# Two-layer deformable-attention kernel: the feed-forward steps and the next segment's preparation at other steps of the hand-written order

## What is computed

```
q    = grouped 1x1 of bn1(x)
off  = tanh(1x1 of gelu(6x6 stride-4 depthwise conv of q)) * 4      # 64 sample points a group
kv   = bilinear sample of bn1(x) at grid + off;  k, v = grouped 1x1 of kv
pos  = query grid - sample points;  f = sign(pos) * log1p(|pos|)    # 1024 x 64 x 2 a group
bias = w3 . relu(w2 . relu(w1 . f + b1) + b2) + b3                  # hidden width 32
attn = softmax(q.k * scale + bias);  x = x + out_w . (attn . v) + out_b
x    = x + mlp_w2 . gelu(mlp_w1 . bn2(x) + mlp_b1) + mlp_b2         # 128 -> 512 -> 128
```

## Time and profile before

| | before |
|---|---|
| median of 3 runs (lowest to highest) | 901.86 us (900.08 to 902.5) |
| the profiled execution: its time / span of its instructions | 902.57 us / 900.7 us |
| busy in the span: PE / ACT / DVE / POOL | 812.3 / 676.0 / 714.7 / 69.1 us |
| ACT_TABLE_LOADs, in all | 28 of 1283 ns |
| DMA queue of the kernel, share of 16 engines | 10.4% |
| TensorE's granted clock, mean | 0.979 |

### The profile page before, as it was taken

How to read it: one execution, slowest core, us unless ns; L and a number is a source line. 1 busy time by engine, 2 the same in 40 slices (tenths; PEclk the granted TensorE clock), 3 DMA queues, 4 the chain that set the end, 5 groups by cost and what they waited for, 6 DMA issues and landing times.

```text
span 900.7 us, 27769 instructions
## 1 busy us (share of the span) xinstructions
PE 812.3 (90%) x12470; PEld 232.4 (26%) x12470; DVE 714.7 (79%) x498; ACT 676.0 (75%) x775; POOL 69.1 (8%) x40
## 2 busy tenths in 40 slices
PE   2299998899999999788999999988999999999997
PEld 1122222222222222222222222222222222222224
DVE  4699798898876688989885868889888668989843
ACT  1368777978786687896877777797777677888863
POOL 2120013210000004030000000302000000000000
PEclk8589999999999999999999999999999999999999
DMA  4310101020020101002020100102002010100000
GB/s 150 80 30 25 28 9 45 7 53 4 14 54 14 50 3 50 9 3 55 3 64 15 49 4 3 50 8 53 4 4 64 14 50 2 50 27 2 2 15 24
DMA packets 23510, 26.77 MB, mean 30 GB/s; under 512 B 15328, under 2 KB 17504, under 8 KB 23392
## 3 DMA queue, kind: packets, MB, share of 16 engines
q1 hardware_dynamic: 23392, 24.99, 10.4%
HBM read 22.79 MB, written 2.08 MB: 28 GB/s over the span
## 4 chain that ended last, share of the span: by engine, by line
PE 42%; issue 39%; ACT 9%; DVE 5%; POOL 5%; DMA 1%; SPq 0%; ACTq 0%; POOLq 0%
PE pair L887 14%; PE scores L905 13%; ACT h L484 5%; PE pair L861 4%; DVE h L638 3%; POOL conv_prod L356 3%; PE pair L1040 2%; POOL big L464 2%; PE scores L916 2%; PE pair L995 1%; PE pair L1013 1%; PE pair L1031 1%; PE scores L1001 1%; ACT big L586 1%; PE pair L940 1%
## 5 line engine op out<-in xcount | busy, mean ns | idle before, releaser
L638 DVE TENSOR_TENSOR h<-hx,hy 128x2048 f32<-128x2048 f32 x256 | 582.1, 2302 | 76.5 <-PE pair L887 72.4
L484 ACT ACTIVATE h<-pair 128x1024 f32<-128x1024 f32 x512 | 517.6, 1024 | 146.9 <-PE pair L861 104.7
L887 PE MATMUL pair<-h,wts 32*32 32x512 f32 x8192 | 300.6, 605 | 20.5 <-DVE h L638 6.1
L905 PE MATMUL scores<-h,wts 128*32 128x512 f32 x2048 | 275.7, 607 | 0.1
L861 PE MATMUL pair<-fy,u_rows 32*128 32x512 bf16 x1024 | 102.6, 387 | 17.1 <-DMA fy<-fy_dram 17.1
L887 PEld LDWEIGHTS pair<-h,wts 32*32 32x32 f32 x8192 | 66.0, 103 | 82.2 <-ACT h L484 34.7
L861 PEld LDWEIGHTS pair<-fy,u_rows 32*128 32x128 bf16 x1024 | 26.4, 91 | 234.4 <-issue 234.4
L905 PEld LDWEIGHTS scores<-h,wts 128*32 128x32 f32 x2048 | 42.2, 108 | 158.0 <-issue 149.2
L356 POOL TENSOR_TENSOR conv_prod<-qpad,wts 128x288 f32<-128x288 f32 x16 | 34.0, 2153 | 417.7 <-ACT qpad L511 417.7
L464 POOL TENSOR_TENSOR big<-big,hat_x 128x512 f32<-128x512 f32 x16 | 32.4, 2054 | 126.6 <-DVE big L736 126.6
L995 PE MATMUL pair<-const,probs 128*128 128x128 f32 x128 | 20.6, 284 | 21.6 <-ACT h L484 20.8
(11 more groups left out here) (101 smaller groups left out, 375.0 us busy)
## 6 DMA issues: line engine op xcount, KB each, us to landing
hx<-features_dram SPq DMA_DIRECT2D x64, 128.0 KB, 2.7
hy<-features_dram SPq DMA_DIRECT2D x64, 128.0 KB, 3.1
wts<-weights_dram SPq DMA_DIRECT2D x2, 960.0 KB, 8.4
att_den<-reciprocals_dram SPq DMA_DIRECT2D x7, 256.0 KB
x<-x_dram SPq DMA_DIRECT2D x2, 512.0 KB, 5.7
fy<-fy_dram SPq DMA_DIRECT2D x64, 6.0 KB
fy<-fy_dram SPq DMA_DIRECT2D x64, 4.0 KB
fy<-fy_dram SPq DMA_DIRECT2D x64, 2.0 KB
```

Of the source, the lines that this page charges most:

```text
L484: emptied("z", 2 * g + j, act.activation(h2[j][g % H2_BUFS][:].rearrange("p r n -> p (r n)"), pair_of("z", 2 * g + j)[:], ACT.Relu))
L638: dve.tensor_tensor(h1[g % H1_BUFS][:].rearrange("p c (y x) -> p c y x", x=W), hx[unit % 2][:, :, t].unsqueeze(2).broadcast_to([128, CT, H ...
L887: ins = pe.matmul(z_of(g, r)[32 * c:32 * (c + 1)], w(l, "w2")[key_rows(r), key_rows(r)], h1[g % H1_BUFS][key_rows(r), c], start=r >= 2, st ...
L905: ins = pe.matmul(scores[phase % 2][32 * r:32 * (r + 1)], w(l, "w3")[:, 32 * t:32 * (t + 1)], h2[rows[0] // 2][step % H2_BUFS][:, r % 2], ...
```

## The change

Two of the tables get other numbers, and the entries of the perceptron become a table of their own with three rows, so that the two query halves of a segment can have different steps. Arithmetic, tiles and instructions stay the same.

```diff
 BEFORE_SLOTS = {
-    ("dve", "norm1", 0): 28, ("pe", "q", 0): 28, ("act", "q_out", 0): 28, ("pool", "conv_products", 0): 31,
+    ("dve", "norm1", 0): 32, ("pe", "q", 0): 32, ("act", "q_out", 0): 32, ("pool", "conv_products", 0): 35,
...
 AFTER_SLOTS = {
     ("pe", "attend", 0): 5, ("act", "attend_out", 0): 5, ("dve", "reciprocal", 0): 9, ("dve", "divide", 0): 12,
-    ("pe", "project", 0): 12, ("dve", "residual1", 0): 14, ("pe", "mlp_up", 0): 14, ("act", "mlp_gelu", 0): 14,
-    ("pe", "mlp_up", 1): 15, ("act", "mlp_gelu", 1): 15, ("pe", "mlp_down", 0): 17, ("dve", "residual2", 0): 19,
+    ("pe", "project", 0): 12, ("dve", "residual1", 0): 14,
 }
+MLP_SLOTS = [{
+    ("pe", "mlp_up", 0): up, ("act", "mlp_gelu", 0): up, ("pe", "mlp_up", 1): up + 1, ("act", "mlp_gelu", 1): up + 1,
+    ("pe", "mlp_down", 0): down, ("dve", "residual2", 0): down + 2,
+} for up, down in ((21, 27), (15, 21), (14, 17))]
...
-        for (engine, stage, part), step in AFTER_SLOTS.items():
+        mlp = MLP_SLOTS[2 if half >= LAST - 1 else half % 2]
+        for (engine, stage, part), step in [*AFTER_SLOTS.items(), *mlp.items()]:
```

More of the change, by code:

```diff
@@ L76 @@
 BEFORE_SLOTS = {
-    ("dve", "norm1", 0): 28, ("pe", "q", 0): 28, ("act", "q_out", 0): 28, ("pool", "conv_products", 0): 31,
[L78 to L87, removed]
+    ("dve", "norm1", 0): 32, ("pe", "q", 0): 32, ("act", "q_out", 0): 32, ("pool", "conv_products", 0): 35,
+    ("pool", "conv_products", 1): 35, ("dve", "conv_products", 0): 35, ("dve", "conv_products", 1): 36,
+    ("pe", "image_t", 0): 35, ("act", "image_t_out", 0): 35, ("dve", "conv_sum", 0): 37,
+    ("dve", "conv_sum", 1): 38, ("act", "conv_gelu", 0): 37, ("pe", "offset", 0): 38,
+    ("act", "offset_tanh", 0): 38, ("dve", "positions", 0): 41, ("pe", "spread", 0): 40,
+    ("act", "features", 0): 40, ("act", "spread_out", 0): 40, ("dve", "features_sign", 0): 43,
+    ("act", "distances", 0): 42, ("act", "distances", 1): 43, ("act", "distances", 2): 44,
+    ("act", "distances", 3): 45, ("dve", "hats", 0): 46, ("dve", "hats", 1): 48,
+    ("pool", "hat_products", 0): 46, ("pool", "hat_products", 1): 48, ("dve", "hat_products", 0): 49,
+    ("dve", "hat_products", 1): 50, ("pe", "sample", 0): 52, ("dve", "sample_out", 0): 54,
+    ("pe", "keys_values", 0): 55, ("act", "keys_values_out", 0): 55,
 }
@@ L130, in plan @@
     parts = {}
-    for (engine, stage, part) in list(BEFORE_SLOTS) + list(AFTER_SLOTS):
+    for (engine, stage, part) in [*BEFORE_SLOTS, *AFTER_SLOTS, *MLP_SLOTS[0]]:
         parts[engine, stage] = max(parts.get((engine, stage), 0), part + 1)
```

## The result

The changed kernel takes **902.79 us** (median of 12 runs, 901.41 to 906.0) against 901.84 (12 runs, 900.08 to 903.15): a ratio of 1.0019, 95% interval 1.001 to 1.0027. That is within 0.3%, if anything slightly slower, and not the forecast 897.8. The profiled execution took 902.18 us with a span of 900.4.

A forecast was written before the change was run, and what follows sets the result against it. PE sets the pace in undisturbed phases, so an ACT load counts only where PE waits for ACT. Per segment -0.2 - 0.8 - 1.0 + 1.3 - 0.9 = -1.6, three times -4.8 from 902.57: 897.8 us; range 890.5 to 904.

The forecast's parts named there:

- The gain is eaten in steps 42 to 50: Rival: crowded steps 43 and 44 delay the last hats, POOL's products hold h tiles; +0.5 a segment, 901 to 904; chance 0.23.
- Preparation, DVE and POOL: I take 0, in between: Hats to last products: POOL's products may each hold an h tile 1.08 us; bounds -1.9 to +2.1 a segment, taken as 0.
- the sign that the prediction had named for this: Phase 6 or 7: PE waiting over 2 us a segment for DVE's h tiles would show the DVE term wrong.
- Perceptron, -0.2: Phases 1 to 3: one Gelu wait gone, -0.4; less cover at steps 14 and 16, +0.2; together -0.2 us a segment.
- one wait of PE for Gelus: Sign: PE's waits at L892 for Gelus would be one of about 0.4 us a segment, at step 14.
- step 12's load: Step 12's Exp loses its table load, taken as hidden behind a `project` on PE: 0, up to -0.8 us.
- Exp's load 0.8: Step 36's Exp on ACT loses its table load: -0.8 us a segment.
- `conv_gelu` 1.0: Load and Gelu move from step 33 to 37: -0.5 for room on ACT, -0.5 for PE's wait; together -1.0 us.
- Copies of keys and values, -0.9: The five copies stood behind the widened maxima, costing 1.7 us; at step 55 0.75 is left: -0.9 a segment.
- Distances, +1.3: ACT's distances, two a step, move from steps 39 to 42 to 42 to 45 with less room: 2.1 becomes 3.4 us.
- Starved POOL, 911: Rival: DVE without idle in steps 47 to 52 starves POOL's products, PE waits at step 52; 911 us; chance 0.12.
- All loads in full, 891: Rival: all nine removed table loads come back at 1.283 us each, 11.5 us, giving 891; chance 0.15.

The follow-up runs named there:

- e6: Changed kernel with the distances of the three preparations in the loop cut from 512 to 16 columns, rest left out: 904.05 us.
- e3: Changed kernel with POOL's four hat products a segment cut from 512 to 16 columns, rest left out: 894.25 us.
- e8: Kernel before the change with POOL's four hat products a segment cut from 512 to 16 columns, rest left out: 899.39 us.
- e5: Changed kernel with all eight hat products on DVE and none on POOL, result whole: 898.58 us.
- e1: Kernel before the change with only the perceptron's new steps, preparation as before: 902.23 us.
- e7: Changed kernel with distances, hats, products, sample and keys and values at later steps (hats at 51 and 53), POOL's products kept: 897.14 us.
- e10: Changed kernel with hats at 51 and 53, POOL's products kept, and the perceptron at its steps of before, six loads more: 895.29 us.
- e9: Changed kernel with hats at 51 and 54 and all hat products on DVE, two at each of steps 53, 55, 56, 57: 892.98 us.
- e11: Changed kernel with hats at 51 and 54, all hat products on DVE, and the perceptron at its steps of before: 891.94 us.
- e2: Kernel before the change with only the preparation's new steps, perceptron as before: 902.36 us.

## Why the prediction was wrong

The range held the time and the forecast did not. What came true is the rival "The gain is eaten in steps 42 to 50", priced at 901 to 904; of its two reasons the holds came, and the crowded ACT did not set the length (e6). That its +0.5 a segment is met so closely is partly luck: by the phases POOL's products cost 1.5 more a segment, not 2.1, and the perceptron's 0.4 makes up most of the rest. Step by step:

- **The failed step is "Preparation, DVE and POOL: I take 0, in between".** The term measured its upper bound or near it: 4 x 1.08 = 4.3 us of DVE held, against 0.2 + 1.0 + 1.1 = 2.3 before (the scaling of hx and hy, 0.97 and 1.77 where 0.80 and 0.74 are normal, and one h tile), so 2.0 more where the upper bound was 2.1. In time that is 1.5 a segment by the phases and 2.0 by the medians. Phases 6 and 7 came out at 9.3 instead of 7.8. (By the forecast's own terms, 6.9 + 1.3 - 0.9, it would have been 7.3; its phase lengths spread the same sum otherwise.) PE's waits for DVE at step 51 (2.26 and 3.05 in two of three segments) are the sign that the prediction had named for this, though PE waited for the maximum that stands behind the held h tiles in DVE's queue and not for a tile. The reason given for the middle, "the work is the same", was no reason. DVE's timeline of the kernel before, segment 1, while POOL's products run (390.3 to 398.2):

```profile
393.87 0.69 DVE L765 TENSOR_REDUCE neg_max<-pair 128x8 f32<-128x512 f32 x1 [1.34 <-PE pair L995]
394.48 0.97 DVE L758 TENSOR_SCALAR hx<-hx,wts 128x1024 f32<-128x1024 f32 x1
395.36 1.77 DVE L759 TENSOR_SCALAR hy<-hy,wts 128x1024 f32<-128x1024 f32 x1
```

There DVE stood idle for 1.34 us, waiting for PE, and one of the four products held nothing; between the moved hats and `sample` DVE has no idle, and all four do. The text itself counted two more h tiles between hats and products, which was the evidence for the upper end. Shown by e3 and e8 together, and by e5 and e6.
- *Perceptron, -0.2.* It is +0.2: phases 1 to 3 are 21.1 over, 20.9 before. The mechanism held: one wait of PE for Gelus is left, 0.30 at step 14 (forecast about 0.4), and step 12's load was hidden: phases 2 and 3 are not below 17, and from one L887 to the next step 12 takes the same 4.12 before and after. Mis-sized by 0.4 a segment, which sits in steps 16 and 21; what lengthens them I did not isolate. That it is no gain is seen three times, each within the intervals but of the same sign: e1 has a ratio 0.0005 above before, e7 0.0006 above e10, e9 0.0009 above e11.
- *Exp's load 0.8 and `conv_gelu` 1.0.* Confirmed as a sum: phase 4 is 2.06 (forecast 1.9), phase 5 6.31 (6.4), and e2 shows the same two numbers. Other stages move between these phases too, and no run takes the two terms apart.
- *Copies of keys and values, -0.9.* Confirmed: from one L887 to the next, step 51 before took 4.12, 1.70 over an empty step; step 55 after takes 4.07, 0.79 over the 3.28 that step 55 took before.
- *Distances, +1.3.* The crowding is there, but it isn't what sets the end (e6). With POOL's term it is not a sum but a maximum: the later of two delays is paid.
- *Starved POOL, 911.* Did not happen: `sample` does not wait for POOL. A row of DVE without idle, from 181 to 209 in segment 0, was not enough, because POOL got its turn there after each of DVE's instructions. As a mechanism the rival is not refuted: in the kernel before, POOL's half of `conv_products` did starve beside a DVE without idle (the last section has the rows).
- *All loads in full, 891.* Refuted: ACT is busy for 10.4 us less, and the time is the same. The 2.66 us a switch of the Trainium skill (ScalarE: Activation LUTs, What ACT_TABLE_LOAD costs), by which it would have been an estimated 879, shows in no run here.

Summed up, the phases of segment 1 give +0.5, three times that +1.6, and +1.3 if each segment's own phases are added up, where -4.8 was forecast. That the profiled executions differ by -0.4 has two reasons outside the change: phase 5 of segment 2 before has 0.8 of low clock in it, and step 25 of segment 0 begins 0.8 earlier after, which varies by about as much from run to run.

## What to carry to other kernels

Work taken off an engine is worth its price only in the steps where that engine is the one waited for; take the windows of those steps, not the sum over the span, and where two engines are late in the same steps count the later one and not both. Before you move a stage, list what will run beside it at the new place and look for idle time there: POOL's products cost more, not less, when the idle time of DVE that they had used was gone, and a few short products on DVE itself, one step each, were cheaper than "free" ones on POOL. An engine that runs ahead needs its inputs that many steps earlier: here DVE leads ACT by two.

## What the runs showed of the hardware

**POOL and DVE exclude each other by whole instructions, and mostly take turns.** In the kernel after, each POOL product of 128x512 lengthened exactly one DVE instruction by 1.08 us, h tiles of two inputs and hats of one input alike (1.23 to 2.29), and waited itself for one of DVE's. Taken one by one, the four of segment 0 last 3.24, 3.32, 2.26 and 3.33 us: 1.0 more than the h tile (2.28) or the hats (1.23) that ran ahead of them. The Trainium skill (SBUF — State Buffer, SBUF: two separate sides) calls it an exclusive lock, and these rows agree; who gets the next turn it does not say. Among the hat products the two engines alternate. They don't always: POOL's and DVE's rows of the kernel before, segment 1, where POOL makes its half of `conv_products`:

```profile
347.04 9.95 POOL L356 TENSOR_TENSOR conv_prod<-qpad,wts 128x288 f32<-128x288 f32 x4 [163.63 <-ACT qpad L511]
```

```profile
357.02 1.35 DVE L668 TENSOR_REDUCE conv<-conv_prod 128x32 f32<-128x1152 f32 x1 [3.02 <-POOL conv_prod L356]
```

The first of these four products takes 7.65 us, the others 0.82 and less. DVE runs six instructions in that time, all of normal length, and POOL is through 0.7 us after DVE has nothing left to do; then DVE stands 3.02 us waiting for POOL. What decides between turn and starving, no run here shows. The advice of the Trainium skill that work moved between the two "might not help" (Perfetto Trace Analysis, Optimizing Scalar/DVE Operations) fits e5, where taking POOL's share back to DVE gained 4.2 us.

**A short wait of PE can be followed by microseconds at half its clock.** PE's timeline in the kernel after, segment 1, and the window of that stretch (granted clock third from the end):

```profile
398.40 1.07 PE L910 MATMUL scores<-h,wts 128*32 128x512 f32 x8
399.40 0.39 PE L866 MATMUL pair<-fy,u_rows 32*128 32x512 bf16 x2
401.45 0.41 PE L866 MATMUL pair<-fy,u_rows 32*128 32x512 bf16 x2 [1.66 <-ACT h L489]
402.36 2.02 PE L892 MATMUL pair<-h,wts 32*32 32x512 f32 x32 [0.50 <-ACT h L489]
```

```profile
401.69:408.52 6.83, 6.33 (x78) 0.90 (x76) 6.83 (x3) 4.79 (x6) 6.83 (x3) 0.50 0.75 167
```

PE had worked for a dozen us with no gap over 0.4, waited 1.66 us for ACT, and from 401.69 the granted clock is 0.5 (1.2 GHz) for 6.83 us; the same 32 matmuls of L892 take 2.02 us instead of 1.17. It cost nothing here, because DVE was later still. It need not happen: in segment 2 of the same execution PE waits 1.66 us at the same place and 3.05 us for the maximum, and the clock stays at 1.00 in both windows (602.19:627.65 and 627.65:655.13 above). In e2 the low clock comes behind the wait for DVE, its timeline of PE and the window in segment 0:

```profile
206.27 1.15 PE L887 MATMUL pair<-h,wts 32*32 32x512 f32 x32 [3.06 <-DVE neg_max L765]
```

```profile
207.70:211.10 3.40, 3.40 (x44) 0.41 (x36) 2.91 (x2) 2.33 (x3) 0.00 (x0) 0.50 0.00 0
```

There nothing hides the 3.4 us, and phases 6 and 7 are 10.7 to 10.8 over in that profile instead of 9.3. So a wait of PE is sometimes paid twice, which no term of the forecast had. e11 shows no such stretch from 52 us to the end of its span.
